# Cross attention on one Trainium2 core: scores as plain fp32 over 32 channels in row groups, outputs masked and folded by a matmul

## The reference, cut

```python
# queries = layernorm(x) [128, 32, 128]; keys = values = ctx [128, 257, 128]; mask [32, 257]
q = queries.reshape(B, L, 16, 8)          # 16 heads of 8 channels
k = keys.reshape(B, S, 16, 8)
v = values.reshape(B, S, 16, 8)
scores = jnp.einsum('blhe,bshe->bhls', q, k)
A = jax.nn.softmax(scores / sqrt(8), axis=-1) * mask      # masked after the softmax
out = jnp.einsum('bhls,bshd->bhld', A, v).reshape(B, L, -1)
x = x + out                               # then self attention, then the experts
```

## Time and profile before

| | us |
|---|---|
| median of 3 runs | 1140.04 (1138.3 to 1141.13) |
| span of the profiled execution | 1137.9 |
| first to last maximum of the cross attention | 21.2 to 608.4 |
| one half (8 steps), mean of 20 | 18.42 |

### The profile page before, as it was taken

The page is one execution under the profiler, slowest core; times in us unless marked ns, Lnnn a source line. Parts: engine busy times, 40 slices in busy tenths (PEclk is TensorE's granted clock), DMA queues, the critical chain, the costliest instruction groups (busy, mean ns, idle before and its releaser), DMA issues. The chain is left out here.

```text
span 1137.9 us, 28862 instructions
## 1 busy us (share of the span) xinstructions
PE 1012.6 (89%) x8140; PEld 912.4 (80%) x8140; DVE 924.6 (81%) x2376; ACT 706.3 (62%) x2102; POOL 617.8 (54%) x694
## 2 busy tenths in 40 slices
PE   4999999999999999999996788887889898888983
PEld 3888888888888888888885787887878787787873
DVE  6787887878787887878885788878659999999995
ACT  3565656666555666566653667666557777676774
POOL 7444454535454554545441444445347887777786
PEclk9999999999999999999998898989999999999997
DMA  2321111111111111111140000000000000000000
GB/s 67 83 78 45 50 50 46 48 49 42 49 43 47 46 44 50 50 44 50 49 140 1 1 1 0 0 0 0 1 2 6 5 9 5 9 9 5 9 5 15
DMA packets 40743, 35.59 MB, mean 31 GB/s; under 512 B 7628, under 2 KB 36360, under 8 KB 40712
## 3 DMA queue, kind: packets, MB, share of 16 engines
q1 hardware_dynamic: 40712, 35.21, 11.5%
HBM read 24.69 MB, written 2.10 MB: 24 GB/s over the span
## 5 line engine op out<-in xcount | busy, mean ns | idle before, releaser
L598 ACT ACTIVATE E<-SC,neg_max 128x257 f32<-128x257 f32 x512 | 237.9, 472 | 137.0 <-DVE neg_max L678 135.5
L454 PE MATMUL SC<-Kt,Qbd 128*128 128x258 f32 x1024 | 293.8, 410 | 16.1 <-ACT Kt L579 13.4
L454 PEld LDWEIGHTS SC<-Kt,Qbd 128*128 128x128 f32 x1024 | 245.9, 310 | 35.7 <-ACT E L598 20.6
L678 DVE TENSOR_REDUCE neg_max<-SC 128x2 f32<-128x514 f32 x256 | 175.6, 686 | 76.3 <-PE SC L454 74.7
L686 DVE TENSOR_TENSOR Et<-ETP,mask_T 128x512 f32<-128x512 f32 x256 | 173.7, 679 | 8.9 <-PE ETP L468 7.2
L468 PE MATMUL ETP<-ident,E 128*128 128x128 f32 x1024 | 156.2, 275 | 0.9 <-ACT E L598 0.9
L1436 PE MATMUL PO<-W,hid 128*128 128x128 f32 x1024 | 138.2, 278 | 18.8 <-ACT hid L1477 18.8
L1436 PEld LDWEIGHTS PO<-W,hid 128*128 128x128 f32 x1024 | 131.5, 192 | 29.0 <-issue 21.6
L1501 ACT ACTIVATE Y<-Z,zb,zs 128x128 f32<-128x128 f32 x256 | 111.1, 486 | 59.9 <-DVE zb L1656 59.9
L1425 PE MATMUL PH<-xT,W 128*128 128x256 f32 x512 | 135.1, 387 | 0.5 <-ACT xT L1469 0.5
L316 POOL TENSOR_TENSOR V_split<-V,ones 128x256 fp32r<-128x256 f32 x128 | 93.3, 729 | 66.5 <-DMA V<-in_ctx_dram 66.5
(11 more groups left out here) (170 smaller groups left out, 1859.7 us busy)
## 6 DMA issues: line engine op xcount, KB each, us to landing
V<-in_ctx_dram SPq DMA_DIRECT2D x64, 256.0 KB, 2.8
Qbd<-Qt SPq DMA_DIRECT2D x256, 32.0 KB, 2.0
xh<-in_x_dram SPq DMA_DIRECT2D x32, 64.0 KB, 2.3
last_rep<-in_ctx_dram SPq DMA_DIRECT2D x128, 2.0 KB
X<-in_x_dram SPq DMA_DIRECT2D x32, 64.0 KB
out_dram<-Xo SPq DMA_DIRECT2D x64, 32.0 KB, 1.5
W<-in_L_ffn_w_dram SPq DMA_DIRECT2D x1, 1024.0 KB
W<-in_L_ffn_w_dram SPq DMA_DIRECT2D x2, 512.0 KB
```

Of the source, the lines that this page charges most:

```text
L454: i = pe.matmul(SC[s % 2][:, u, 0:S + 1], Qbd[:, j // HB, u, :, (2 * x + s % 2) * HB + j % HB], Kt[:, j % 4, s % 2, :], start=(x == 0), st ...
L598: i = act.activation(E[:, h, u0 + u, :], SC[s % 2][:, u, 0:S], ACT.Exp, bias=neg_max[:, s % 2, u:u + 1], accum_out=den[:, h, u0 + u:u0 + u ...
L678: dve.tensor_reduce(neg_max[:, s % 2, :], SC[s % 2][:, :, 0:S], AX.X, ALU.max, negate=True).then_inc(max_sb, 1)
```

## The change

- **Scores.** No fp32r and no split. `Kt` and `Qbd` are plain fp32 with 8 partitions a head. Group g of 4 heads lies on partitions 32g to 32g + 31, and its score matmul uses only these: one matmul of 257 columns over 32 partitions for each group, two a step, in two different row groups of the array. (`Qbd` still has zeros where head and query block differ, within 32 partitions.)
- **Keys.** No `split` on POOL. `turn_keys` turns two batches with four transposes, straight from `V`; `keep_keys` copies both at once. Twice a half in place of four times. `place_last` on DVE: once a half, four columns.
- **Queries.** One pair of transposes; one ACT copy; POOL builds `Qbd` by one multiplication with `hh_scaled` (128 x 512). The 256 DMAs of `place_queries`, the second `keep_queries` on DVE, `K_last`, `split_last` and the zeroing of `Qbd` go away.
- **Outputs.** `keep_sums` moves from ACT to DVE and multiplies `AV` by the head mask into `O_m` (128 x 512), one step later in its order. `turn_out` is four fp32 matmuls with the constant `gather_d` (32 columns each) in place of four transposes; `own_outputs` is one DVE instruction of 128 x 128 in place of four of 32 x 128.
- The order of `steps` on PE, ACT, DVE and POOL follows: keys at steps 2 and 6 of a half, queries at step 0.

The diff, cut to its core (the new `place_queries` is POOL's, the new `keep_sums` DVE's):

```diff
-                    for u in range(2):
-                        for x in range(2):
-                            i = pe.matmul(SC[s % 2][:, u, 0:S + 1], Qbd[:, j // HB, u, :, (2 * x + s % 2) * HB + j % HB],
-                                          Kt[:, j % 4, s % 2, :], start=(x == 0), stop=(x == 1))
+                    for u in range(2):
+                        g = 2 * (s % 2) + u
+                        r = slice(32 * g, 32 * g + 32)
+                        i = pe.matmul(SC[s % 2][:, u, 0:S], Qbd[r, h, jj, :], Kt[r, h, jj, 0:S], start=True, stop=True)
                     i.then_inc(sc_ps, 1)
...
-                    for p in range(2):
-                        for k in range(KT):
-                            c = (KT * p + k) * P
-                            i = pe.transpose(MISC[:, c:c + P],
-                                             V_split[:, j % 4, k, 8 * p:8 * p + 8, :, :].rearrange("p g x c -> p (g x c)").bitcast(F32),
-                                             ident[:, :])
+                    for j in range(2):
+                        for a in range(KT):
+                            c = (KT * j + a) * P
+                            i = pe.transpose(MISC[:, c:c + P], V[:, 2 * k + j, a, :], ident[:, :])
                     i.then_inc(kt_ps, 1)
...
+                    pe.transpose(MISC[:, 0:P], xn[:, :], ident[:, :])
+                    pe.transpose(QT_LAST[:, :], last_rep[:, h, :], ident[0:n, 0:n]).then_inc(qt_ps, 1)
...
                     for j in range(HB):
-                        i = pe.transpose(MISC[:, P * j:P * j + P], O_c[:, j, :], ident[:, :])
+                        i = pe.matmul(MISC[:, 32 * j:32 * j + 32], O_m[:, j, :], gather_d[:, :, :].rearrange("p g d -> p (g d)"),
+                                      start=True, stop=True)
                     i.then_inc(o_ps, 1)
...
+                def place_queries(t, h):
+                    pool.wait_ge(qt_sb, m + 1)
+                    pool.tensor_tensor(Qbd[:, h, :, :].rearrange("p j (q l) -> p j q l", q=HQ),
+                                       Qt[:, :, :].unsqueeze(2).to_broadcast([P, HB, HQ, L]),
+                                       hh_scaled[:, :, :].unsqueeze(1).to_broadcast([P, HB, HQ, L]), ALU.mult).then_inc(q_bd, 1)
...
+                def keep_sums(t, h):
+                    dve.wait_ge(av_full, m + 1)
+                    dve.tensor_tensor(O_m[:, :, :].rearrange("p j (q l) -> p j q l", q=HQ),
+                                      AV[:, :, :].rearrange("p j (q l) -> p j q l", q=HQ),
+                                      hh_of[:, :].unsqueeze(1).unsqueeze(3).to_broadcast([P, HB, HQ, L]), ALU.mult).then_inc(o_m, 1)
```

More of the change, by code:

```diff
@@ L193, in _ @@
             def _(sp):
-                def place_queries(t, h):
-                    sp.wait_ge(q_lo, 2 * t + h + 1)
-                    if isinstance(t, int) and t == 0:
-                        sp.wait_ge(q_zero, 2)
-                    for u in range(2):
-                        for q in range(HQ):
-                            r = slice(64 * u + 16 * q, 64 * u + 16 * q + 16)
-                            sp.dma_start(Qbd[r, h, u, L * q:L * q + L, :].bitcast(F32), Qt[r, :, :].bitcast(F32)).then_inc(q_in[h], 16)
                 def load_residual(q):
@@ L386, in _ @@
                 pool.memset(Vbd[:, :, :], 0.0).then_inc(pool_set2, 1)
-                split(0, 2, first=True)
-                split(0, 3, first=True)
                 run_tiles(steps, pool)
@@ L729, in steps @@
                     for s in range(STEPS):
-                        q = (t, 1) if s < HSTEPS else (t + 1, 0)
-                        more = not (final and s >= HSTEPS)
                         if not final and s % HSTEPS == 4:
@@ L736, in steps @@
                         maxima(t, s, first=fresh and s < 2)
-                        if more and s % HSTEPS == 1:
-                            keep_queries(*q)
-                        if s % 2 == 0:
-                            if s < STEPS - 2:
-                                place_last(t, s // 2 + 1, first=fresh and s < 6)
-                            elif not final:
-                                place_last(t + 1, 0)
+                        if s % HSTEPS == 4 and not (fresh and s < HSTEPS):
+                            keep_sums(*((t, 0) if s > HSTEPS else (t - 1, 1)))
                         if not final and s % HSTEPS == 4:
@@ L748, in steps @@
                             keep_probs(tt, ss, first=fresh and s < 6)
+                        if s % HSTEPS == 0 and not (final and s >= HSTEPS):
+                            place_last(*((t, 1) if s < HSTEPS else (t + 1, 0)))
                         if not final and s % HSTEPS == 4:
@@ L783, in _ @@
                 normalise(0, 0, first=True)
-                dve.memset(Qbd[:, 0, 1, :, :].bitcast(F32), 0.0).then_inc(q_zero, 1)
-                keep_queries(0, 0)
-                place_last(0, 0, first=True)
+                place_last(0, 0)
                 norm_stats(0, 1)
```

224 lines of the change are left out of this document (75 added, 149 removed).

## The result

The changed kernel takes **1429.37 us** (median of 4 runs, 1427.01 to 1431.41); the kernel before, in the same series, 1139.17 (1137.72 to 1141.13). The ratio is 1.2536, 95% interval 1.2509 to 1.2562: a quarter slower where 8% faster was forecast, and outside the range. The answers of the profile after to the earlier trace rows first: busy time by engine on the page, then its groups (line, engine, operation, count | busy us, mean ns | idle time ahead of them), then the cross attention's stretch in the columns of the earlier trace rows.

What follows compares the result with a forecast made beforehand. PE was taken to set the cross attention's step nearly alone; a half falls from 18.42 to 15.56 us, less 0.1 of waits, over 32 halves 88 us, plus 3 at the start: 1049 us, range 1036 to 1108.

Steps and rivals of the forecast that it cites:

- the granted clock falls: Rival: fewer array rows working lower PE's clock to 0.90; 1.7 us a half, 55 us, 1104 us; chance 0.03.
- Slower: Outcome that the changed kernel takes longer than the kernel before; chance 0.13.
- Scores: PE's score group a step: two row groups run at once in two rounds, 0.635 us.
- no overlap: Rival: row groups' score records run one after another, 1.06 us a group; 1160 us; chance 0.14.
- weight loads take turns: Rival: second row group's weight load waits for the first's, 0.11 us a step; 28 us, 1077 us; chance 0.12.
- strict order of records: Rival: score records start and end in program order, three rounds, not two; 56 us, 1105 us; chance 0.05.
- Other PE terms: PE's groups besides scores: transposes 0.585 us, weighted values 0.57, outputs 1.03; a half 15.56 us in all.
- The wait for the exponentials: PE's weight loads waiting for ACT, about 0.55 us a half before the change, would go.
- DVE's order: Rival: DVE binds around steps 4 to 6, 0.9 us of waits a half; 27 us, about 1076 us; chance 0.08.
- The sum: 2.76 us saved in each of 32 halves, 88 us, plus about 3 us at the start: 1049 us.
- The start: Before the first scores: without POOL's zeroing of `Qbd` and the splits, about 3 us earlier (0 to 5).

Runs made afterwards that it cites:

- before_rows32: Kernel before the change, its fp32r score matmuls cut to 32 of 128 rows, other rows' products left out; 1101.87 us (1 run).
- keys_twice: Changed kernel with each group of four key transposes written twice, the second over the first; 1095.26 us (1 run).
- loads_moved: Changed kernel with a burst of 6 whole-array matmuls at step 4 and the first 16 residual loads behind the next queries' load; 1418.21 us.
- burst_once: Changed kernel with 28 plain fp32 whole-array matmuls, once, at step 14 of the first tile; 1072.23 us (1 run).
- burst_early: Changed kernel with 28 whole-array fp32 matmuls, once, at step 4 of the first tile instead of step 14; 1438.95 us (1 run).
- burst_short: Changed kernel with 6 whole-array fp32 matmuls, once, at step 14 of the first tile; 1066.23 us (1 run).
- full_rows: Changed kernel with plain fp32 scores over all 128 rows, other head groups' rows zeroed by POOL; 1110.32 us, ratio 0.9723 to the kernel before.
- mixed: Changed kernel with scores over all 128 rows at odd steps and in 32-row groups at even steps; 1081.11 us, ratio 0.9474 to the kernel before.
- after_fp32r: Changed kernel with score operands rounded to fp32r, one record a matmul; 1008.46 us (1 run).
- both variants of the kernel before: Kernel before with score matmuls on 32 of 128 rows, as fp32r (1101.87 us) or read as plain fp32 (1228.05 us), 1 run each.
- filler_turn: Changed kernel with one added whole-array fp32 transpose of the values ahead of each step's scores; 1513.31 us, ratio 1.3267 to the kernel before.
- burst_timed: burst_once timed again in three rounds; 1073.7 us, ratio 0.9402 to the kernel before.
- fp32r_timed: after_fp32r timed again in rounds; 1008.26 us, ratio 0.8836 to the kernel before.

## Why the prediction was wrong

**The step that failed** is the rival "the granted clock falls". It was given 0.03 and 55 us, by the mean of 0.90 in self attention, and set aside with "PE has no gaps". Both halves of that were wrong. The clock has two levels, and the 0.90 of self attention is a mean over stretches at either; the changed loop stands at one of them all through. At the lower one a half takes 27.75 us, not 17.3. And the absence of gaps says nothing for the upper level: PE was busy 820.00 of 820.00 us at the lower one. Worked out again with the measured halves, the term is 32 x (27.75 - 15.5) = 392 us; 1429.4 less that is 1037 us, 12 us from the forecast. "Slower" had a chance of 0.13, nearly all of it for row groups that don't overlap; it came by another cause. What the forecast took for granted is that the array stands at the level of the earlier trace rows. The kernel before rose at 29.6 us and didn't fall again in the stage; the changed loop, once at 1.2 GHz, never rises by itself.

The Trainium skill, "TensorE: Matmul & The Clock Gate", section "What's actually happening", ties the level to how busy the engine has been: idle leads to the lower level, sustained activity to the upper. The fourteen falls beside gaps in the table agree. The falls of before_rows32, with no gap over 0.8 us, and the 820 us without a gap at 1.2 GHz don't, if "busy" is read as the profile's busy time.

Point by point, at 2.4 GHz:

- *Scores*, 0.635 us: right, 0.63 (keys_twice). Row groups overlap, in two rounds. The rivals "no overlap", "weight loads take turns" and "strict order of records" are settled against: two starts 0.007 us apart, then two more 0.32 us after the first. (The working of "no overlap" has the same term as 3.4 and as 3.49 us a half; by its own sizes it is 3.4, so that rival stood 3 us too high.) The row column of the records reads 32*128, so the matmuls do run as row groups.
- *Other PE terms*: transposes 0.585 (0.59), weighted values 0.57 (0.57), outputs 1.03 (1.01: the fold of loads_moved starts at 49.33 and the next scores at 50.34), a half 15.56 (15.50 in burst_once). Right, and not by errors that cancel: summed over 20 halves of burst_once, a half has scores 5.09 us (forecast 5.08), turned probabilities 4.45 (4.53), weighted values 2.41 (2.28), keys 1.02 (1.02), key 257 1.09 (1.20), queries 0.42 (0.42), outputs 1.01 (1.03).
- *The wait for the exponentials* is gone: right; PE is busy 473.64 of 476 us in burst_once, and in 16 halves of it (200 to 448.2 us) no weight load of the scores waits for them; those of the turned probabilities do for 5.7 us, hidden behind running matmuls. What had held PE itself at that place in the kernel before was the copy of the keys, which stands behind the exponentials on ACT: 8.8 us in 20 halves, ended by L579, so 0.44 us a half where 0.55 was priced.
- *DVE's order*: right in that it doesn't bind. Its load was put too high: 372.20 us of 476 are 12.1 us a half, where 13.9 was worked out, and 78% where 88% was named. The working added durations, and successive ones overlap: in burst_early a maximum starts at 64.93 us and the masked copy behind it at 65.52, though the maximum's record is 0.68 us long.
- *The sum.* burst_short takes 1066.2 us, and its first two halves, partly at 1.2 GHz and with 4.98 us of burst, take 50.7 us where two at full clock take 31.0: 1066 - 20 = 1046 us against 1049. So the sum was right for a level that the kernel doesn't reach by itself.
- *The start*, 3 us earlier: the first maximum of burst_short, of which nothing differs up to there, stands at 19.0 us in place of 21.2; 2.3 us, inside the 0 to 5.

What stays open: why the changed loop doesn't rise by itself when those of full_rows, mixed, after_fp32r and both variants of the kernel before do. Neither row groups alone nor plain fp32 in them explain it, and whole-array work added evenly doesn't change it, whatever its data. How the whole-array groups bunch may count (keys_twice against filler_turn); that isn't shown, and no run here gives a rule.

The best version with full fp32 here is burst_short (1066.23 us, one run); timed in rounds is burst_timed, 6% under the kernel before. With rounded score operands fp32r_timed takes 1008.26 us.

## What to carry to other kernels

Before pricing an edit that leaves the array partly idle, ask at which of its two clock levels the new loop will run and what brings it there; which of two steady states a loop runs in can be decided before it begins, and the busy share need not show it (PE: 100% at 1.2 GHz, 99.5% at 2.4). Read the level from the pace of an instruction that hasn't changed, such as a transpose, before explaining any single group. If everything on TensorE is slower by the same factor, try one short burst of whole-array matmuls behind the last wait of the start, and if the level is lost again, look for a gap near the fall.

## What was not expected of the hardware

- The same instructions in the same order take 15.5 or 27.75 us a half, and keep to either for over 450 us. A single burst (4.98 us in burst_short) decides it.
- More work made the kernel faster by 334 us (keys_twice) or slower by 84 us (filler_turn), with as many added transposes, 8 a half, in rows of four or one by one.
- In the changed loop the factor between the levels is 27.75 / 15.5 = 1.79, though the clocks differ by 2. Single transposes differ by 0.213 / 0.109 = 1.95, scores by 1.16 / 0.635 = 1.83, weighted values, with a change of shape on both sides, by 1.01 / 0.57 = 1.77.
- A faster loop finds a wait where the slower one finds none, and the level falls inside it: the gap of 8.48 us in burst_early comes from 16 loads queued ahead of one that the loop needs sooner.
